# Keys' even and odd latent lanes of two units in separate banks, rotated by sums on GpSimd; keys loaded in halves

## What is computed

```
q_lat = q @ q2l_w.T + q2l_b
k_lat = k @ kv2l_w.T + kv2l_b
v_lat = v @ kv2l_w.T + kv2l_b
q_lat = q_lat * cos + _rotate_half(q_lat) * sin
k_lat = k_lat * cos + _rotate_half(k_lat) * sin
q_for_k = q_lat @ wqk_w.T + wqk_b
att = jnp.einsum('bhql,bhkl->bhqk', q_for_k, k_lat) * L ** (-0.5)
```

## Time and profile before

| what | value |
|---|---|
| median of three runs | 2801.23 us (2798.45 to 2801.73) |
| profiled execution, its own time | 2801.95 us |
| its span, first to last instruction | 2800.1 us |
| busy share: TensorE, VectorE, ScalarE, GpSimd | 97%, 75%, 64%, 29% |
| projection / attention | to about 360 us / about 366 to 2052 us |

### The profile page before, as it was taken

One profiled execution on the slowest core, in us unless ns is written; L12 is line 12 of the kernel. 1 busy time (PEld: TensorE's weight loads), 2 busy tenths in 40 slices (PEclk: granted clock), 3 DMA queues, 4 the chain that ended last, 5 costly groups with the idle time before them and its releaser, 6 DMA issues. The chain is left out here.

```text
span 2800.1 us, 46944 instructions
## 1 busy us (share of the span) xinstructions
PE 2705.5 (97%) x16154; PEld 1868.7 (67%) x16154; DVE 2102.7 (75%) x5498; ACT 1790.8 (64%) x3325; POOL 799.2 (29%) x761
## 2 busy tenths in 40 slices
PE   8999989999999999999999999999999997899995
PEld 7888855656565566666655565656457775799994
DVE  7888879888888888888888888888545554454575
ACT  5666625767777777766777776777654453555575
POOL 7888820100100100100110110110015555122255
PEclk9999979999999999999999999999999999899998
DMA  6878863234344333442432531551054440443455
GB/s 222 280 265 281 284 184 88 65 84 112 83 102 105 92 89 80 111 103 62 116 97 62 122 92 32 122 130 40 24 165 162 143 126 27 102 97 93 117 161 171
DMA packets 251214, 342.32 MB, mean 122 GB/s; under 512 B 46942, under 2 KB 133255, under 8 KB 249696
## 3 DMA queue, kind: packets, MB, share of 16 engines
q1 hardware_dynamic: 232160, 311.82, 39.3%
q0 software_dynamic: 18816, 27.50, 4.4%
HBM read 194.68 MB, written 155.06 MB: 125 GB/s over the span
## 5 line engine op out<-in xcount | busy, mean ns | idle before, releaser
L1047 ACT ACTIVATE att_probs<-att_score_bank 128x512 f32<-128x512 f32 (+1 forms) x2240 | 1127.2, 595 | 461.4 <-PE att_score_bank L990 451.2
L1094 DVE TENSOR_REDUCE att_partial_max<-att_max_bank 128x1 f32<-128x512 f32 x1536 | 979.8, 682 | 174.5 <-PE att_max_bank L976 173.0
L1076 POOL TENSOR_SCALAR_AFFINE_SELECT att_probs<-att_probs 128x512 f32<-128x512 f32 x256 | 162.8, 638 | 1499.6 <-ACT att_probs L1047 1499.5
L990 PE MATMUL att_score_bank<-att_q_st,att_k_st 98*128 98x512 f32 (+3 forms) x1792 | 578.7, 381 | 7.8 <-DMA att_q_st<-att_max_rows 6.0
L976 PE MATMUL att_max_bank<-att_k_st,att_q_st 96*128 96x512 f32 (+3 forms) x1792 | 570.3, 374 | 1.3 <-DVE att_partial_max L1094 0.8
L1007 PE MATMUL att_acc_bank<-att_probs,att_v_st 128*32 128x512 f32 (+3 forms) x5120 | 528.6, 536 | 0.0
L1100 DVE CUSTOM_DVE_ANT_0 att_edge_sum<-att_max_bank,first_edge 128x256 f32<-128x256 f32 (+3 forms) x1024 | 459.7, 483 | 66.9 <-PE att_max_bank L976 64.7
L990 PEld LDWEIGHTS att_score_bank<-att_q_st,att_k_st 98*128 98x128 f32 x1792 | 319.7, 190 | 164.9 <-ACT att_probs L1047 81.2
L976 PEld LDWEIGHTS att_max_bank<-att_k_st,att_q_st 96*128 96x128 f32 x1792 | 329.6, 190 | 136.6 <-DVE att_partial_max L1094 52.5
L1007 PEld LDWEIGHTS att_acc_bank<-att_probs,att_v_st 128*32 128x32 f32 x5120 | 136.3, 109 | 248.2 <-issue 140.4
L288 POOL TENSOR_TENSOR proj_op_low<-proj_turned,proj_op_high 128x512 fp32r<-128x512 f32 x192 | 244.3, 1297 | 47.2 <-ACT proj_op_high L448 44.7
(11 more groups left out here) (252 smaller groups left out, 4303.4 us busy)
## 6 DMA issues: line engine op xcount, KB each, us to landing
qk_parts<-proj_parts SPq DMA_DIRECT2D x64, 1024.0 KB, 5.2
att_k_st<-qk_parts SPq DMA_DIRECT2D x168, 256.0 KB, 6.6
att_q_st<-qk_parts SPq DMA_DIRECT2D x159, 256.0 KB, 4.6
v_tokens<-proj_v_tok SPq DMA_DIRECT2D x64, 256.0 KB, 4.6
att_v_st<-v_tokens SPq DMA_DIRECT2D x64, 256.0 KB, 7.5
y_heads<-kept_y_raw SPq DMA_DIRECT2D x64, 256.0 KB, 2.3
exp_w<-in_ew SPq DMA_DIRECT2D x16, 1024.0 KB, 8.3
first_q<-qk_parts SPq DMA_DIRECT2D x33, 256.0 KB, 4.4
```

Source lines behind the costliest of these rows:

```text
L990: last = nc.tensor.matmul(score_ps[h % SCOREB][:, i * (CH - q0):(i + 1) * (CH - q0)], k_tile(g, kt // TT)[:, j + i, (kt % TT) * P:(kt % TT ...
L1047: nc.scalar.activation(probs[:, k % PROBS, j:j + heads, q0:CH], score_ps[h % SCOREB][:, 0:heads * (CH - q0)].rearrange("p (j n) -> p j n", ...
L1076: nc.gpsimd.affine_select(out=block_probs, in_=block_probs, pattern=[[0, HG], [1, P]], compare_op=ALU.is_ge, fill=zero, base=0, channel_mu ...
L1094: nc.vector.tensor_reduce(partial_max[:, m % 2, j * TT + t, kb:kb + 1], bank[:], AX.X, ALU.max).then_inc(unit_reduced, 1)
```

## The change

The keys' latent lanes are laid out anew. The columns of the folded key weight are permuted so that a pair of units shares two banks: the bank of the even unit holds the even lanes of both, that of the odd unit the odd lanes of both. A lane and its partner then lie on the same partition of two banks, and rotating is an element-wise difference or sum: even lanes cos - odd lanes sin, and odd lanes cos + even lanes sin. VectorE still makes the four products of a unit; the two of a key go into `k_terms`. GpSimd adds them (`whole_k`) into the SBUF tile `k_whole`, in place of the third low half. The matmuls with `rot_r`, the sum `add_k`, the third conversion on ScalarE and the bank `fin_k` in that role are gone; `high_k` and `low_k` read `k_whole` in place of `fin_k`. Queries get their lanes permuted inside the unit (the weights are permuted on the host's side of the inputs), which moves no instruction.

Since a stored key plane now holds half the lanes of two units, a load of a unit's keys takes 16 partitions from each unit of its pair: six DMAs of 16 partitions in place of three of 32. The waits for a load count nine or ten DMAs where they counted six or seven.

```diff
 def load_qk(sp, d, n, q, k, done):
     g, c = divmod(n, NC)
-    src = d["qk"].rearrange("s c f (j p) n -> s c f p j n", p=L)
-    for dst, f in ((q[0:L], 0), (q[L:2 * L], 0), (q[2 * L:3 * L], 1), (k[0:L], 2), (k[L:2 * L], 3), (k[2 * L:3 * L], 2)):
-        sp.dma_start(dst.bitcast(F32), src[g, c, f]).then_inc(done, 16)
+    q_src = d["qk"].rearrange("s c f (j p) n -> s c f p j n", p=L)
+    for dst, f in ((q[0:L], 0), (q[L:2 * L], 0), (q[2 * L:3 * L], 1)):
+        sp.dma_start(dst.bitcast(F32), q_src[g, c, f]).then_inc(done, 16)
+    k_src = d["qk"].rearrange("s c f (u j i) n -> s c f u i j n", j=HG, i=L // 2)
+    for at, f in ((0, 2), (L, 3), (2 * L, 2)):
+        for odd in range(2):
+            dst = k[at + odd * L // 2:at + (odd + 1) * L // 2]
+            sp.dma_start(dst.bitcast(F32), k_src[g - g % 2 + odd, c, f, g % 2]).then_inc(done, 16)
...
+            def whole_k(c):
+                odd, terms = c % 2, k_terms[:, c // 2 % 2]
+                pool.wait_ge(roped, 4 * (c + 2 - odd))
+                if c >= 2:
+                    pool.wait_ge(k_split, c - 1)
+                nc.gpsimd.tensor_tensor(k_whole[:, odd], terms[:, odd, 0], terms[:, 1 - odd, 1],
+                                        ALU.add if odd else ALU.subtract).then_inc(k_added, 1)
...
             for c in range(UNITS):
-                for i in range(3):
-                    pool.wait_ge(highs_done, 3 * c + i + 1)
+                for i in range(2):
+                    pool.wait_ge(highs_done, 2 * c + i + 1)
...
+                if c >= 1:
+                    whole_k(c - 1)
                 if c % G == 1 and c // G + 1 < XCHUNKS:
                     low_x(c // G + 1)
+            whole_k(UNITS - 1)
...
                 if c == UNITS - 2 * G:
                     sp.wait_ge(parts_out[0], 16)
+                    sp.wait_ge(parts_out[1], 16)
                     load_qk(sp, d, 0, first.q, first.k, first.loaded)
...
+                        for odd in range(2):
+                            last = nc.tensor.matmul(paired[:, g // 2, odd, g % 2], ck[:, g, at],
+                                                    fold_k[:, odd * 64:(odd + 1) * 64], start=True, stop=True)
...
-                pe.wait_ge(lows_done, 3 * c + 3)
-                if c >= 1:
-                    pe.wait_ge(k_split, c)
-                product(fin_k[:], [(rot_r[:], high[:, 2]), (rot_r[:], low[:, 2])]).then_inc(fin_k_ready, 1)
...
-                nc.scalar.activation(parts[:, c % PARTS, 2], fin_k[:], ACT.Copy).then_inc(k_high_done, 1)
+                nc.scalar.activation(parts[:, c % PARTS, 2], k_whole[:, c % 2], ACT.Copy).then_inc(k_high_done, 1)
...
-            def add_k(c):
-                dve.wait_ge(fin_k_ready, c + 1)
-                nc.vector.tensor_tensor(fin_k[:], fin_k[:], k_cos[:, c % OPS], ALU.add).then_inc(k_added, 1)
...
-                nc.vector.tensor_tensor(parts[:, c % PARTS, 3], fin_k[:], parts[:, c % PARTS, 2].bitcast(F32),
+                nc.vector.tensor_tensor(parts[:, c % PARTS, 3], k_whole[:, c % 2], parts[:, c % PARTS, 2].bitcast(F32),
                                         ALU.subtract).then_inc(k_split, 1)
```

More of the change, by code:

```diff
@@ L339, in fold @@
             def fold(x, k):
-                c_w, fold_w = ((cq, fold_q), (ck, fold_k))[x]
+                paired = lat[1][k][:].rearrange("p (pair odd u n) -> p pair odd u n", pair=G // 2, odd=2, u=2)
                 for g in range(G):
-                    last = nc.tensor.matmul(lat[x][k][:, g * P:(g + 1) * P], c_w[:, g, k * P:(k + 1) * P],
-                                            fold_w[:], start=True, stop=True)
+                    at = slice(k * P, (k + 1) * P)
+                    if x == 0:
+                        last = nc.tensor.matmul(lat[0][k][:, g * P:(g + 1) * P], cq[:, g, at], fold_q[:], start=True, stop=True)
+                    else:
+                        for odd in range(2):
+                            last = nc.tensor.matmul(paired[:, g // 2, odd, g % 2], ck[:, g, at],
+                                                    fold_k[:, odd * 64:(odd + 1) * 64], start=True, stop=True)
                 last.then_inc(folded, 1)
@@ L353, in _ @@
             nc.tensor.matmul(fin_q[:, 0:G], fold_q[:], b_cq[:], start=True, stop=True)
-            nc.tensor.matmul(fin_q[:, G:3 * G], fold_k[:], b_ck[:], start=True, stop=True).then_inc(folded, 1)
+            for u in range(2):
+                for odd in range(2):
+                    for pair in range(2):
+                        at = G + 2 * pair + odd
+                        nc.tensor.matmul(fin_q[64 * u:64 * (u + 1), at:at + 1], fold_k[:, odd * 64:(odd + 1) * 64],
+                                         b_ck[:, 2 * pair + u:2 * pair + u + 1], start=True, stop=True)
+            nc.tensor.matmul(fin_q[:, 2 * G:3 * G], fold_k[:], b_ck[:, G:2 * G], start=True, stop=True).then_inc(folded, 1)
             pe.wait_ge(weights_done, SCALED)
-            nc.tensor.matmul(fin_k[:, 0:P], rot[:, 0], wqk_scaled, start=True, stop=True).then_inc(folded, 1)
+            nc.tensor.matmul(fin_k[:, 0:P], rot, wqk_scaled, start=True, stop=True).then_inc(folded, 1)
             def product(out, terms):
@@ L444, in high_op @@
             def high_op(c, i):
-                act.wait_ge(roped, 4 * c + (1, 2, 4)[i])
+                act.wait_ge(roped, 4 * c + i + 1)
                 if c >= OPS:
-                    act.wait_ge(fin_k_ready if i == 2 else fin_q_ready, c - OPS + 1)
+                    act.wait_ge(fin_q_ready, c - OPS + 1)
                 nc.scalar.activation(op_high[:, c % OPS, i], turned[:, c % 2, i], ACT.Copy).then_inc(highs_done, 1)
@@ L2267, in laid_out @@
     bias = w["L0_attn_c_attn_b"]
+    lanes = np.arange(P).reshape(HG, L // 2, 2)
+    split = lanes.transpose(2, 0, 1).reshape(-1)
+    within = lanes.transpose(0, 2, 1).reshape(-1)
+    biases = {n: np.tile(w[f"L0_attn_{n}_b"], HG) for n in ("q2l", "kv2l", "wqk")}
+    k_bias = w["L0_attn_kv2l_b"]
     return {
```

75 lines of the change are left out of this document (37 added, 38 removed).

## The result

| | before | after |
|---|---|---|
| median of three runs | 2801.23 us | 2837.17 us (2832.70 to 2838.06) |
| ratio | | 1.0131, 95% interval 1.0116 to 1.0147 |
| span of the profiled execution | 2800.1 us | 2835.4 us |
| first latent matmul of 512 columns starts | 15.41 us | 20.49 us |
| mean chunk of the projection | 20.84 us | 22.62 us |

The chunk is measured from the start of GpSimd's subtraction for x in one chunk to that in the next, over the fourteen steps from the second to the sixteenth. The forecast of 2801.4 us and its range, up to 2817, were wrong. The 35.3 us of the two spans divide into 27.3 ahead of attention's first maxima and 8.0 behind it.

The account below looks back on a forecast made before the run. TensorE was taken to bound the kernel, GpSimd the projection after the change. Projection -12.5, start +4.5, loads +8.0, early load +0.5, projection's end -0.3 sum to +0.2 on 2801.95 us profiled: median 2801.4, range 2784 to 2817.

Parts of the forecast that it names:

- The projection: Projection: two matmuls fewer a unit free 29.1 us of TensorE, but GpSimd's chunk of 20.39 us limits the gain to 12.5.
- VectorE waits out the running instruction: Projection: VectorE's two-SBUF-input subtraction waits for one GpSimd instruction, then GpSimd's next loses 0.45 us a unit.
- GpSimd becomes the bound: Projection: with VectorE's holds GpSimd's chunk goes from 18.59 to 20.39 us, above TensorE's 19.21.
- the slower rival: Projection: each VectorE subtraction also waits a whole GpSimd instruction, 1.26 us, so the projection gains nothing: 2814 us; chance 0.23.
- VectorE leads GpSimd by almost two units of buffers: Projection: the argument against VectorE's waiting 1.26 us a subtraction and starving GpSimd, which would give 2814 us.
- If nothing else came to the front, a chunk would take 19.21: Projection: TensorE's chunk of 21.03 us loses 1.82 with two matmuls fewer a unit.
- ScalarE at nothing: Projection: ScalarE loses one conversion a unit and gets a wait for GpSimd's sum; counted as no change, covered by idle 30%.
- The start: Weight and bias folds: 32 added passes at 0.21 us, 6.7 us, less 0.33 and 1.9: +4.5, bounds 1.2 and 6.4.
- the credit of 1.9 us for a higher clock: Start: the first nine latent matmuls, begun after 20 us, would run at TensorE's upper clock level, 1.9 us less.
- The loads: Attention: key loads in halves of 16 partitions cost 2.0 us at each of four waits, +8.0, between 0 and 14.4.
- the ring: Projection: three engines above 85% in one ring of waits, the argument for 2814 us.
- The engines do not meet: Projection: VectorE's subtraction falls in GpSimd's gaps or the lock spares the sum, TensorE stays the bound: 2785 us; chance 0.17.

Follow-up runs that it names:

- the version with joined halves: The changed kernel with whole key planes loaded in three DMAs again and three stores a unit in place of one: 2906.03 us, ratio 1.0373.
- the halves alone: The kernel before, with its three key DMAs of a load split into six of 16 partitions each, same data: 2813.98 us, ratio 1.0053.
- the copy to PSUM: The changed kernel, with ScalarE copying the sum of the keys into the free PSUM bank, where VectorE's low half reads it: 2790.34 us, ratio to before 0.9969.

## Why the prediction was wrong

**The projection (forecast -12.5, measured +22.4: 27.3 less the 4.9 by which the tenth latent matmul is later).** The step that failed is "VectorE waits out the running instruction". It was read from one place, and for the subtraction that place could not tell one instruction from a run of them. GpSimd's next row there, which the forecast did not look at, is:

```profile
25.93 3.82 POOL L288 TENSOR_TENSOR proj_op_low<-proj_turned,proj_op_high 128x512 fp32r<-128x512 f32 x3 [1.96 <-ACT proj_op_high L448]
```

The instruction that VectorE waited out at 23.98 was also the last before a pause of 1.96 us. In the loaded stretch GpSimd has no pause for up to five instructions, and VectorE waited for three or five in 13 of the 64 units: 2116 ns on average over the stretch, where the forecast looked for 1 to 1.8 us. The Trainium skill's page "SBUF — State Buffer", section "Who interferes with whom", names this pair of engines and operands, and its summary has the later one blocked "until the first finishes". The trace agrees that the two exclude each other, and in 14 units that the wait is for one instruction; it doesn't agree on the order or the length in a unit like the one shown, where VectorE's listed start (103.62) is the earlier (GpSimd's is 103.71), and where it waited until 109.97 though the first of the five finished at about 105.

From that follow the other misses. "GpSimd becomes the bound" was wrong: its hold by VectorE is 0.29 us a unit for the 0.45 forecast (its subtractions' means rise from 1297 to 1397 ns, its x subtraction's from 2421 to 2804: 18.5 us over 64 units). One hold costs what was forecast, 0.36 to 0.55 us, but 47 of its instructions were held and not 64. It stands idle waiting for VectorE's products, and it is VectorE that has no time left. The reason given against the slower rival, "VectorE leads GpSimd by almost two units of buffers", doesn't help where the wait is longer than a unit.

**What the forecast priced well.** "If nothing else came to the front, a chunk would take 19.21": with the lock away it takes 19.21 us, and GpSimd at 18.59 us by the forecast is hidden behind it, as said. ScalarE at nothing was right as far as the runs go, even with a copy more.

**The start (forecast +4.5, measured 4.8 to 5.1).** The size is right by two errors that cancel. The sixteen added bias passes cost 0.10 us each where 0.21 was taken, 1.8 us less; and the credit of 1.9 us for a higher clock never came, since the first nine latents are 0.43 us apart there too, and only 0.2 us of it were gained (the nine take 3.82 us, 20.49 to 24.31, for 3.99 in the earlier trace rows).

**The loads (forecast +8.0, measured 8.0 in the changed kernel and 11.2 alone).** The price of one load was right, and the sum right by luck. The opening wait grew by 2.04 us (7.05 for 5.01), which is the forecast's 2.0 a load. But the forecast has four such waits, and the four together grew from 8.0 us to 10.8, by 2.8:

```profile
PEld att_max_bank L995 <- DMA att_v_st<-v_tokens: 10.8, 4, 7.6
```

Where the other 5.2 us lie is open. 1.9 of them stand ahead of a score matmul, in a wait that the profile gives no releaser and that the kernel before doesn't have. And TensorE's clock, which was not in the sum, is lower in the first 60 us of attention; before the change, and after:

```profile
366.42:426.42 60.00, 54.24 (x212) 32.59 (x212) 51.61 (x156) 17.40 (x34) 17.94 (x10) 0.71 0.57 133
```

```profile
393.69:453.69 60.00, 50.59 (x170) 31.24 (x170) 45.21 (x137) 14.51 (x28) 17.29 (x9) 0.61 0.72 132
```

That the clock is a cause is not shown: the version with joined halves has 0.65 there and loses nothing behind the first maxima. What is shown is that the halves cost something: the five kernels with them whose traces are compared here take 2441.7 to 2448.5 us from the first maxima on, the five with whole planes 2433.7 to 2434.3. The rate did not halve: 131 GB/s where the two units' halves are fetched, 156 to 160 with the halves alone, against 205 to 213. The Trainium skill's same page, "Door 1: The DMA port swizzle", gives 104 and 189 GB/s for these two widths, in transfers of 1 MiB; both measured rates are higher, and their order agrees. (The keys' extra time by these figures is 3.4 us, where the prediction has 3.5.)

**The rivals.** The slower one ("VectorE is held as well") had the mechanism and the ring, and priced it at one GpSimd instruction, 1.26 us; with up to 6.9 us in one unit of a chunk its 2814 became 2837. "The engines do not meet" is what the copy to PSUM makes true: 2790 for the rival's 2785.

**Still open.** Why VectorE gets in after one GpSimd instruction in 14 units and waits for three or five in 13, and which instant decides, was not tried. Ten of the eleven longest waits were issued 0.06 to 0.11 us ahead of the first GpSimd instruction behind the x load's issue (103.62 and 103.71 in the unit shown), the eleventh 0.04 behind that start. Of the 14 that got in, 13 were issued 0.79 to 1.01 us into a GpSimd instruction of 1.29, but one issued 0.99 into such an instruction waited for five (5.82 us). Why the halves of two units load more slowly (131 GB/s) than the two halves of one (156) is not settled either.

## What to carry to other kernels

Where VectorE runs beside a busy GpSimd, give each of its subtractions and sums at most one SBUF input (the cast of the earlier trace rows, with one, ended 0.28 us behind a GpSimd instruction, so a cast may need a test of its own): a sum that lay in PSUM and is moved to SBUF can cost more than the matmuls it saves, here 51 us against 29. If two can't be avoided, bound the wait by the longest run of GpSimd without a pause, not by one of its instructions, and put a pause where VectorE needs its turn. A layout that splits a plane into halves of fewer partitions can cost time at every load on the path; look for an order of lanes that lets the pieces lie in one stride.

## What the runs showed of the hardware that was not expected

- VectorE's subtraction with two SBUF inputs waited in 13 of 64 units for three or five GpSimd instructions that follow each other (up to 6.96 us for 0.68), and in 14 others got its turn between two such instructions, after one.
- Sixteen f32 passes with one moving column and 64 weight columns took 1.39 us (18.14 to 19.53), 0.09 each, where passes with 64 or 128 moving columns and 128 weight columns took 0.22.
